# Attention tiles with a second score product that has keys standing and queries moving, and the expert weights of two other blocks kept resident

## What is computed

```python
def _expert(x, Wqkv, bqkv, Wo, bo, g1, be1, W1, bf1, W2, bf2, g2, be2):
    q, k, v = (to_heads(t) for t in jnp.split(x @ Wqkv.T + bqkv, 3, axis=-1))   # 8 heads of 32
    attn = jax.nn.softmax(jnp.einsum('bhqd,bhkd->bhqk', q * scale, k), axis=-1)
    ctx = jnp.einsum('bhqk,bhkd->bhqd', attn, v).transpose(0, 2, 1, 3).reshape(b, s, d) @ Wo.T + bo
    x = _layernorm(x + ctx, g1, be1)
    h = gelu(x @ W1.T + bf1); h = gelu(h @ W2.T + bf2)
    return _layernorm(x + h, g2, be2)
```

## Time and profile before

| | |
|---|---|
| median of three runs | 3118.02 us (3117.1 to 3120.5) |
| profiled execution | 3119.24 us, span 3117.5 us |
| mean granted clock of PE | 0.891 |
| busy share | PE 79%, DVE 50%, ACT 37%, POOL 17% |
| attention tiles (tx) | 1642 to 2765 us |
| tiles of the fourth block (sro) | 1242 to 1350 us |
| tiles of the eighth block (nee) | 2988 to 3086 us |

### The profile page before, as it was taken

The page is one execution under the profiler, slowest core; times in us unless marked ns, Lnnn a source line. Parts: engine busy times, 40 slices in busy tenths (PEclk is TensorE's granted clock), DMA queues, the critical chain, the costliest instruction groups (busy, mean ns, idle before and its releaser), DMA issues. The chain is left out here.

```text
span 3117.5 us, 52757 instructions
## 1 busy us (share of the span) xinstructions
PE 2457.1 (79%) x18627; PEld 2058.2 (66%) x18627; DVE 1568.1 (50%) x3095; ACT 1143.3 (37%) x2211; POOL 522.6 (17%) x818
## 2 busy tenths in 40 slices
PE   6979589769977748875785999999888998964256
PEld 4858589769956634764784777777777777744244
DVE  3636512232236741143444776777776777742355
ACT  2323222112213211122223656665656566624422
POOL 0000022122202100510001111122221122110043
PEclk9989699779978969987897999999999999976678
DMA  4000023124341101730565231334145452112066
...
DMA packets 147050, 293.50 MB, mean 94 GB/s; under 512 B 37155, under 2 KB 74057, under 8 KB 143717
## 3 DMA queue, kind: packets, MB, share of 16 engines
...
...
## 5 line engine op out<-in xcount | busy, mean ns | idle before, releaser
L2226 PE MATMUL tx_ring<-g_ident,tx_p 128*128 128x128 f32 x2552 | 395.9, 283 | 75.3 <-DVE tx_p_t L2470 35.8
L2226 PEld LDWEIGHTS tx_ring<-g_ident,tx_p 128*128 128x128 f32 x2552 | 287.1, 142 | 178.9 <-DVE tx_p_t L2470 58.6
L2470 DVE COPY tx_p_t<-tx_ring 128x512 f32<-128x512 f32 x464 | 305.7, 684 | 129.6 <-PE tx_ring L2226 126.4
L2463 DVE TENSOR_REDUCE tx_neg_max<-tx_scores 128x1 f32<-128x1354 f32 x232 | 362.0, 1561 | 17.6 <-PE tx_scores L2214 17.6
L2360 ACT ACTIVATE tx_p<-tx_scores,tx_neg_max 128x1354 f32<-128x1354 f32 x232 | 322.8, 1392 | 87.2 <-DVE tx_neg_max L2463 84.7
L2367 ACT ACTIVATE tx_p_t<-tx_ring 128x384 f32<-128x384 f32 x232 | 113.7, 490 | 291.1 <-PE tx_ring L2226 287.3
L2214 PE MATMUL tx_scores<-tx_keys,tx_queries 96*128 96x512 f32 (+1 forms) x696 | 203.2, 401 | 14.9 <-DMA tx_queries<-tx_q_hi 11.2
L2266 PE MATMUL tx_ring<-tx_p_t,tx_values 128*32 128x128 f32 x5104 | 170.7, 295 | 13.2 <-ACT tx_p_t L2367 12.7
L2266 PEld LDWEIGHTS tx_ring<-tx_p_t,tx_values 128*32 128x32 f32 x5104 | 152.9, 119 | 26.7 <-ACT tx_p_t L2367 23.9
L2214 PEld LDWEIGHTS tx_scores<-tx_keys,tx_queries 96*128 96x128 f32 x696 | 115.9, 193 | 25.5 <-issue 14.9
L192 PE MATMUL ln_turned<-g_ident,g_xn 128*128 128x128 f32 x176 | 39.4, 408 | 117.5 <-DVE g_xn L179 117.5
...
## 6 DMA issues: line engine op xcount, KB each, us to landing
...
```

The source lines that it names most:

```text
L2226: last = nc.tensor.transpose(ring[u % 2][:, (t - t0) * P:(t - t0 + 1) * P], p[n % 2][:, t * P:(t + 1) * P], g.ident[:])
L2463: nc.vector.tensor_reduce(neg_max[:, n % 4:n % 4 + 1], sc[n % 2][:, 0:N], AX_X, ALU.max, negate=True)\
L2470: nc.vector.tensor_copy(p_t[:, n % TURNED, t0:t0 + nt, :], ring[u % 2][:, 0:nt * P].rearrange("p (t q) -> p t q", q=P))\
```

## The change

Three things are changed.

**Attention tiles.** There is one score buffer, and the ring has 5 banks. Scores with queries standing are made as before, but only for the maximum. POOL splits minus the maximum into a high part and the rest (`split_maxima`, two 128x1 operations); PE turns the three columns 1, high, rest to rows (`turn_maxima`), ACT copies them to rows 96 to 98 of the queries (`keep_maxima`). A second product, `turned_scores`, 11 f32r matmuls with 99 rows, has keys standing (with 0, 1, 1 in the extra rows; in the 54 columns past the tokens -1e30 stands against the 1) and queries moving, and gives scores less maximum with keys on partitions. ACT takes the exponential of each chunk from the ring to `p_t`. `turn`, the copies and `inverse` are gone. The row sums are made by DVE (`sum_keys`, over the 11 blocks, 128x128 left) and PE (`sums`, 4 products with ones per half tile); DVE takes the reciprocal of 128x128 and multiplies. Scores of a head wait for the maximum of the head ahead. On DVE and ACT some steps change places; POOL's work is laid out by heads. SP waits for the turned product of a head (`full`) where it waited for its scores. `spread` of the returns is told the ring's size.

**Fourth block.** `RoutedWeights` holds affine values, gates, bias, first layers, shared and all 8 expert matrices; SP issues the 14 loads in the norm ahead. PE reads each tile's expert into a register (`owners`) and takes its slice. The loads in the later stages are gone.

**Eighth block.** `NormedWeights` does the same with 33 loads; ACT copies the tile's first matrix (128x512) to `w1_now` (`bring`), and PE, ACT and DVE each read the expert of a tile.

```diff
-            def load(i):
-                k = i % ROUTED_SETS
-                new = dict(cond=expert(i) != expert(i - ROUTED_SETS)) if i >= ROUTED_SETS else {}
-                sync.dma_start(we[:, k, :, :].rearrange("p k o -> p (k o)"),
-                               expert_dram[bass.ds(expert(i), 1)].rearrange("o p n -> p (o n)"), **new).then_inc(we_loaded[k], 16)
...
-                    last = nc.tensor.matmul(row[i % 2][:, 0:D], hg_t[:, i % 2, f, :], we[:, i % ROUTED_SETS, f, :],
+                    last = nc.tensor.matmul(row[i % 2][:, 0:D], hg_t[:, i % 2, f, :], we[:, of(i), f, :].rearrange("p o n -> p (o n)"),
...
+    def load(self, sync):
+        a = self.a
+        sync.dma_start(self.affine[:], a["L1_ffn_affine"]).then_inc(self.affine_loaded, 16)
+        sync.dma_start(self.gates[:], a["L1_ffn_gates"].rearrange("(k p) e -> p k e", p=P)).then_inc(self.gates_loaded, 16)
+        sync.dma_start(self.gate_bias[:], a["L1_ffn_gate_bias"].partition_broadcast(P)).then_inc(self.gates_loaded, 16)
+        for i, name in enumerate(("L1_ffn_shared_in_w", "L1_ffn_expert_in_w")):
+            sync.dma_start(self.w_in[i][:], a[name].rearrange("(k p) o -> p k o", p=P)).then_inc(self.w_in_loaded[i], 16)
+        sync.dma_start(self.ws[:], a["L1_ffn_shared_out_w"].rearrange("(k p) o -> p k o", p=P)).then_inc(self.ws_loaded, 16)
+        for e in range(self.experts):
+            sync.dma_start(self.we[:, e, :, :].rearrange("p k o -> p (k o)"), a["L1_ffn_expert_out_weight"][e])\
+                .then_inc(self.we_loaded, 16)
...
+def owners(eng, plan):
+
+    held = {}
+
+    def of(i):
+        if i not in held:
+            held[i] = eng.value_load(plan.owner[0:1, i:i + 1], min_val=0, max_val=plan.experts - 1)
+        return bass.ds(held[i], 1)
+    return of
...
-TURNED = 5
-PE_EXTRAS = {0: ("inverse1", "values1"), 1: ("output", "turn_rows"), 2: ("queries",), 3: ("turn_middle",), 4: ("inverse0", "values0"),
+TURNED = 6
+RING = 5
+CONSTS = 1
+ROWS_ON_PE = ()
+QM = QR + 3
+FAR = -1e30
+PE_EXTRAS = {0: ("values1", "sums1"), 1: ("turn_rows", "output"), 2: ("queries",), 3: ("turn_middle",), 4: ("values0", "sums0"),
              5: ("first0", "first1"), 6: ("second",)}
...
-                if n >= 2:
-                    pe.wait_ge(exp_done, n - 1)
+                if n:
+                    pe.wait_ge(max_done, n)
                 for k0, w in KCH:
-                    last = nc.tensor.matmul(sc[n % 2][:, k0:k0 + w], queries[:, i % 2, hd, :], keys[:, hd, k0:k0 + w],
+                    last = nc.tensor.matmul(sc[:, k0:k0 + w], queries[0:QR, i % 2, hd, :], keys[0:QR, hd, k0:k0 + w],
...
+            def turn_maxima(n):
+                u = at["maxima", n, 0]
+                free(pe, u)
+                pe.wait_ge(max_split, n + 1)
+                nc.tensor.matmul(ring[u % RING][QR:QM, 0:P], max_parts[:, n % 4, :].bitcast(F32), g.ident[:], start=True, stop=True,
+                                 tile_position=(0, QR)).then_inc(full, 1)
+
+            def turned_scores(i, hd, c):
                 u, n = at["heads", i, (hd, c)], HEADS * i + hd
                 free(pe, u)
                 if c == 0:
-                    pe.wait_ge(exp_done, n + 1)
-                    pe.wait_ge(const_made, 3)
+                    written(pe, at["maxima", n, 0])
+                    pe.wait_ge(const_made, CONSTS)
                 t0, nt = TG[c]
                 for t in range(t0, t0 + nt):
-                    last = nc.tensor.transpose(ring[u % 2][:, (t - t0) * P:(t - t0 + 1) * P], p[n % 2][:, t * P:(t + 1) * P],
-                                               g.ident[:])
+                    last = nc.tensor.matmul(ring[u % RING][:, (t - t0) * P:(t - t0 + 1) * P], keys[:, hd, t * P:(t + 1) * P],
+                                            queries[:, i % 2, hd, :], start=True, stop=True)
...
+                    if hd not in ROWS_ON_PE:
+                        pe.wait_ge(summed, summed_by(i, hd))
+                        last = nc.tensor.matmul(ring[u % RING][HD * lane:HD * (lane + 1), 0:P], ones[:],
+                                                over_keys[:, half, lane, :], start=True, stop=True, tile_position=(0, HD * lane))
...
+                t0, nt = TG[c]
+                nc.scalar.activation(p_t[:, n % TURNED, t0:t0 + nt, :],
+                                     ring[u % RING][:, 0:nt * P].rearrange("p (t q) -> p t q", q=P), ACT.Exp)\
+                    .then_inc(drained["act"], 1)
+
+            def keep_maxima(n):
+                u = at["maxima", n, 0]
+                act.wait_ge(full, u + 1)
+                nc.scalar.activation(queries[QR:QM, n // HEADS % 2, n % HEADS, :], ring[u % RING][QR:QM, 0:P], ACT.Copy)\
+                    .then_inc(drained["act"], 1)
...
+            def sum_keys(n):
+                i, hd = n // HEADS, n % HEADS
+                if hd in ROWS_ON_PE:
+                    return
+                written(dve, at["heads", i, (hd, CH - 1)])
+                if i:
+                    dve.wait_ge(full, at[f"sums{hd // 4}", i - 1, 0] + 1)
+                nc.vector.tensor_reduce(over_keys[:, hd // 4, hd % 4, :], p_t[:, n % TURNED, :, :].rearrange("p t q -> p q t"),
+                                        AX_X, ALU.add).then_inc(summed, 1)
...
+                below = at[f"sums{half}", i, 0]
+                dve.wait_ge(full, below + 1)
                 if i:
                     dve.wait_ge(full, at["output", i - 1, 0] + 1)
-                nc.vector.tensor_tensor(ctx_t[:, half, :], ring[u % 2][:, 0:P], inv_t[:, half, :], ALU.mult)\
-                    .then_inc(drained["dve"], 1)
-                written(dve, u)
+                link(nc.vector.reciprocal(inv_t[:, half, :], ring[below % RING][:, 0:P]))
+                nc.vector.tensor_tensor(ctx_t[:, half, :], ring[u % RING][:, 0:P], inv_t[:, half, :], ALU.mult)\
+                    .then_inc(drained["dve"], 2)
+                written(dve, below)
                 dve.sem_inc(ctx_done, 1)
...
-            nc.gpsimd.memset(minus_half[:], -0.5).then_inc(const_made, 1)
-            for k in range(2):
-                nc.gpsimd.memset(p[k][:, N:NP], 0.0).then_inc(const_made, 1)
-            pool.wait_ge(const_made, 3)
+            own(nc.gpsimd.memset(minus_half[:], -0.5))
+            own(nc.gpsimd.memset(ones[:], 1.0))
+            own(nc.gpsimd.memset(max_parts[:, :, 0:1].bitcast(F32), 1.0))
+            own(nc.gpsimd.memset(keys[0:QR, :, NT:NP].bitcast(F32), 0.0))
+            own(nc.gpsimd.memset(keys[QR:QM, :, :].bitcast(F32), 1.0))
+            own(nc.gpsimd.memset(keys[QR:QR + 1, :, 0:N].bitcast(F32), 0.0))
+            nc.gpsimd.memset(keys[QR:QR + 1, :, N:NP].bitcast(F32), FAR).then_inc(const_made, 1)
+            pool.wait_ge(const_made, CONSTS)
+
+            def split_maxima(n):
+                pool.wait_ge(max_done, n + 1)
+                if n >= 4:
+                    pool.wait_ge(full, at["maxima", n - 4, 0] + 1)
+                own(nc.gpsimd.tensor_copy(max_parts[:, n % 4, 1:2], neg_max[:, n % 4:n % 4 + 1]))
+                nc.gpsimd.tensor_tensor(max_parts[:, n % 4, 2:3], neg_max[:, n % 4:n % 4 + 1], max_parts[:, n % 4, 1:2],
+                                        ALU.subtract).then_inc(max_split, 1)
...
+                for hd in range(HEADS):
+                    if HEADS * i + hd + AHEAD < heads:
+                        split_maxima(HEADS * i + hd + AHEAD)
+                    if hd == 0 and i < tiles:
+                        add_bias(i)
+                    if hd == 1 and 0 < i <= tiles:
+                        inverse_std(i - 1, 0, x1_seen, std1_done)
+                    if hd == 2 and 0 < i <= tiles:
+                        middle_rows(i - 1)
+                    if hd == 3 and i + 1 < tiles:
+                        split_queries(i + 1)
+                    if hd == 4 and i + 2 < tiles:
+                        fetch(i + 2)
+                    if hd == 5 and i >= 2:
+                        inverse_std(i - 2, 1, x2_seen, std2_done)
+                    if hd == 6 and i >= 2:
+                        end_rows(i - 2)
+                    if hd == 7 and i >= 2:
+                        pool.wait_ge(y_done, i - 1)
+                        send_rows(nc, g, plan, y[:, i % 2, :], i - 2).then_inc(stored[i % 2], 16)
...
+        sync.dma_start(self.gate[:], a["L3_ffn_Wg"].rearrange("(k p) e -> p k e", p=P)).then_inc(self.gate_loaded, 16)
+        for e in range(self.experts):
+            sync.dma_start(self.w1[:, e, :, :].rearrange("p k o -> p (k o)"), a["L3_ffn_w"][e, :, 0:KD * D])\
+                .then_inc(self.w_loaded, 16)
+            sync.dma_start(self.w2[:, e, :, :].rearrange("p k o -> p (k o)"), a["L3_ffn_w"][e, :, KD * D:2 * KD * D])\
+                .then_inc(self.w_loaded, 16)
+            sync.dma_start(self.b1[:, e, :], a["L3_ffn_cols"][e]).then_inc(self.small_loaded, 16)
+            sync.dma_start(self.rows[:, e, :, :].rearrange("p r d -> p (r d)"),
```

(15 more changed lines are left out.)

385 lines of the change are left out of this document (167 added, 218 removed).

## The result

The changed kernel takes 3311.57 us (median of 4 runs, 3309.46 to 3312.14), the kernel before 3118.48: a ratio of 1.0617, 95% interval 1.0599 to 1.0636. That is 193 us slower, where 3113 was forecast (5 us faster than before), with a range of 3068 to 3182. The profiled execution spans 3307.7 us against 3117.5, at a mean granted clock of 0.856 against 0.891.

What follows compares the result with a forecast made beforehand. In the attention tiles, over a third of the span, PE has the most work but several links wait for round trips. 3119.2 + 1.5 + 19.5 - 16 - 10 = 3114.2, against the median 3113 us; range 3068 to 3182.

Steps and rivals of the forecast that it cites:

- The sum over keys: Attention tiles, DVE: sum over 11 blocks, 1408 elements at 1.04 ns each, 1.62 us a head.
- Rival D: Attention stage: one or two clock falls more a tile, +1.2 to 2.2 us each tile, say 3160; chance 0.12.
- The rest of the period: Attention tiles: heads sum to 36.9 us a tile, 37.6 with 0.7 for clock falls; +1.5 us over 29 tiles.
- The turned product: Attention tiles, PE: 11 f32r products of 128 columns at 0.113 us each, 1.24 us a head.
- rival C: Attention tiles, PE: turned product costs what f32 costs, 2.37 us, 40.5 a tile; about 3205; chance 0.09.
- rival B: Attention tiles: POOL's pair takes 0.32 or turned products start well under 0.11 apart; 36.3 a tile, 3076 us; chance 0.26.
- the shorter price beside the sum: Attention tiles, PE: the Trainium skill's about 81 ns a product, 11 taking 0.89 us in place of 1.24.
- POOL's pair: Attention tiles: two 128x1 POOL operations between each maximum and PE, 0.54 us, between 0.32 and 0.8.
- The start of the stage: Attention stage's start: two large memsets, 9.4 and 9.0 us, ahead of the first fetch; +19.5 us, between 17 and 24.
- The fourth block: Resident weights there: 13 us of waits and latencies gone, tile loop -3; -16 us, between -25 and +5.
- Rival E: Fourth and eighth blocks' tile loops: register reads on PE cost 1 us and more; 3148 us; chance 0.08.
- The eighth block: Resident weights there: 33 issues +3.5, gate -1.6, loop 2.9 us a tile (-11.6); -10 us, between -17 and +8.

Runs made afterwards that it cites:

- e3: Changed kernel with the sum over keys reading the same 1408 elements in memory order (output not the block's): 3144.79 us.
- e12: Changed kernel with each turned product made twice over the same bank: 3326.89 us.
- e1: Kernel before with only the resident weights of the fourth and eighth blocks, attention tiles as before: 3089.99 us, ratio 0.9906.
- e8: Kernel before with the resident weights of the fourth block alone: 3091.54 us, ratio 0.9917.

## Why the prediction was wrong

*The sum over keys* is the step that failed. It was priced at 1.04 ns an element from the earlier trace rows, both reductions over neighbouring elements, and given no bound from above. The operation added reads at a distance of 128 elements and costs 1.85 (2.60 / 1408). The line of the diff shows that (`"p t q -> p q t"`), and no row of before has such a read, so the price needed an upper bound, as the turned product's had. With 2.60, DVE needs 1.56 + 2.60 in a plain head: more than the chain's 3.48, measured 4.27. Exchanging this one term takes 166.8 of the 193 us away (e3).

*The clock.* Rival D named the mechanism and its direction, at 0.12, as independent of the rest. It was a consequence of the longer head: PE at half clock for 162.1 of 700 us with the sum of 2.60, 44.4 with 1.61. Its share is inside the 166.8. In the heads with values 1.9 to 2.1 us are lost against e3, of which 1.0 is the sum itself and 0.9 to 1.1 the longer wait for the values (2.16 and 2.41 instead of 1.27). The two don't simply add: with the same long sum at full clock (e12) that wait is 0.71 and 0.80, so about 1.5 us in each of these two heads go with the clock, some 3 of the 44.2 us of a tile, as far as e12's added products do not shift the wait themselves.

*The rest of the period.* With the sum at its forecast price a tile takes 38.46 (e3), or 37.63 without falls, against 36.9 (the terms of that sum add up to 36.8). The two heads with values took 5.95 each, not 5.54: values and sums end 2.7 us after the maximum began, not 2.5, with PE's four sums at 0.39 and the turn of the maxima at 0.38 where 0.24 stood, and DVE's steps behind them take 3.2, not 3.04. Falls then add 0.83; I had 0.7. But the tile of before was overrated: 37.55 in the window, 37.00 over the whole stage. So with the sum at its forecast price the tiles cost 1.46 × 29 = 42 us in place of 1.5; e3 as a whole is still 28 us slower than its before (3116.66).

*Terms that held.* The turned product: 11 in 1.45 us with the last one's tail, 0.117 apart (medians, e3 alike), forecast 0.113; rival C, from 0.15 on, falls. No spacing well under 0.11, as rival B and the shorter price beside the sum would have it, is seen. POOL's pair: the second begins 0.27 behind the first,

```profile
1653.93 0.19 POOL L2626 CAST tx_max_parts<-tx_neg_max 128x1 fp32r<-128x1 f32 x1 [12.41 <-DVE tx_neg_max L2496]
1654.20 0.19 POOL L2627 TENSOR_TENSOR tx_max_parts<-tx_neg_max,tx_max_parts 128x1 fp32r<-128x1 f32 x1
```

0.46 in all, against 0.54. With neither link as short as it needed, rival B falls too. The reciprocal took 0.96 against 1.16, plain heads 3.46 and 3.56 in e3, forecast 3.48. The query stack delayed nothing that shows. The start of the stage:

```profile
1614.07 9.48 POOL L2617 MEMSET tx_keys<- 3x11264 f32 x1
1623.61 9.12 POOL L2618 MEMSET tx_keys<- 1x10832 f32 x1
...
1633.52 1.03 POOL L1545 DMA_INDIRECT tx_xg<-token_rows,te_source  x1 [0.27 <-POOL tx_keys L2619]
```

9.48 and 9.12 where 9.4 and 9.0 stood, and +17.5 us to the first maximum (forecast +19.5). This is the best predicted term, read from the earlier trace rows.

*The fourth block* gained 26.3, not 16. The latencies came as worked out (13, measured 18.5 to the first expert product, 5.3 of it the late trace). The loop was undersized: windows of its tiles and of the eighth block's,

```profile
1250.20:1319.00 68.80, 64.14 (x339) 54.67 (x340) 11.88 (x28) 16.12 (x27) 47.51 (x49) 1.00 0.44 133
3193.00:3268.00 75.00, 62.74 (x359) 49.72 (x358) 47.49 (x147) 43.97 (x127) 45.00 (x46) 0.99 0.28 84
```

2.46 us a tile in place of 2.85, for which I had allowed 0.1. The DMA share went from 0.78 to 0.44, and with it DVE's waiting for landed returns from 58.0 to 41.2 us; that the loads' absence caused this is the likely reading, no run tests it. The register read on PE delays little: in 18 of 28 tiles the product starts 0.11 us after the last turn ahead of it, with no gap. Rival E falls.

*The eighth block.* 2.9 us a tile was right (first to last product 81.5 / 28 = 2.91), but the tile of before was 3.11 (87.2 / 28) and not 3.3, which was the stage's length over its tiles and contained its start. So 5.7 and not 11.6 were to be had, and the 33 issues in the norm's block took 3.9 back (forecast 3.5 less 1.6). Issue by issue:

```profile
3128.00 0.37 SPq L2733 DMA_DIRECT2D new_gate<-in_L_ffn_Wg  x1
3128.43 0.46 SPq L2735 DMA_DIRECT2D new_w<-in_L_ffn_w  x1
3128.94 0.42 SPq L2737 DMA_DIRECT2D new_w<-in_L_ffn_w  x1
```

about 0.47 apart. The net was 0.4 us between e1 and e8.

*The chances.* Slower had 0.43, and none of its cases named the mechanism that decided; D had the clock, but with one or two more falls a tile and not with a longer head. The range was drawn from the bounds of the other terms, so it had no room for it.
